# Gated linear attention with a feed-forward layer on one core: gate logits through their 16 columns, and five mended waits and passes

## The reference

```
q, k, v = x @ Wq, x @ Wk, x @ Wv          # 4 heads, 64 features for q and k, 128 for v
gl = x @ gk_w1 @ gk_w2 + gk_b             # gk_w1 256x16, gk_w2 16x256
g = log_sigmoid(gl) / 16
S = exp(gt)[:, None] * S + kt[:, None] * vt[None, :];  o_t = qt @ S     # scan over tokens
o = o * rsqrt(mean(o * o) + EPS) * rms_w;  o = o * silu(x @ Wg);  return o @ Wo
x = x + layernorm(attn(layernorm(x)))
x = x + layernorm(gelu(layernorm(x) @ w1 + b1) @ w2 + b2)
```

## Time and profile before

| what | value |
|---|---|
| median of 3 runs | 1352.19 us (1351.74 to 1352.67) |
| the profiled execution | 1351.44 us, its span 1349.6 us |
| PE busy | 1214.3 us (90%) |
| DVE busy | 1040.2 us (77%) |
| ACT busy | 735.0 us (54%) |
| POOL busy | 641.1 us (48%) |
| granted TensorE clock, mean | 0.964 of full speed |
| a pair of passes in the middle | 160.3 us (from 465.19 to 625.55 at the same step) |

### The profile page before, as it was taken

How to read it: one execution, slowest core, us unless ns; L and a number is a source line. 1 busy time by engine, 2 the same in 40 slices (tenths; PEclk the granted TensorE clock), 3 DMA queues, 4 the chain that set the end, 5 groups by cost and what they waited for, 6 DMA issues and landing times.

```text
span 1349.6 us, 24454 instructions
## 1 busy us (share of the span) xinstructions
PE 1214.3 (90%) x8644; PEld 1028.7 (76%) x8644; DVE 1040.2 (77%) x2436; ACT 735.0 (54%) x1571; POOL 641.1 (48%) x877
## 2 busy tenths in 40 slices
PE   5698998989989898998989899898998989999877
PEld 4577787868878787887878778786887868878766
DVE  3759687797868869688786978779686886968773
ACT  5364646656475565646556464665546555474423
POOL 5346353564435544554445635356444554545441
PEclk9889899999999999999999999999998999999998
DMA  2100010100101001020011001010010100101000
GB/s 94 36 32 17 1 56 9 51 17 17 48 1 53 15 17 47 5 63 1 17 48 52 17 0 55 10 52 16 17 48 1 52 17 17 48 1 52 1 17 16
DMA packets 31784, 38.34 MB, mean 28 GB/s; under 512 B 2448, under 2 KB 29104, under 8 KB 31664
## 3 DMA queue, kind: packets, MB, share of 16 engines
q1 hardware_dynamic: 31136, 36.25, 8.3%
q10 hardware_dynamic: 528, 0.52, 0.1%
HBM read 28.38 MB, written 8.39 MB: 27 GB/s over the span
## 4 chain that ended last, share of the span: by engine, by line
PE 47%; DVE 25%; POOL 10%; issue 10%; ACT 8%; DMA 0%; DVEq 0%; POOLq 0%; SPq 0%; ACTq 0%
PE ps_big L262 6%; PE ps_level L262 5%; PE ps_big L263 5%; DVE q_blockdiag L645 5%; PE ps_big L264 5%; PE ps_level L263 5%; PE ps_level L264 5%; DVE attn_T L615 4%; POOL rstd L1197 4%; PE ps_out L476 3%; PE ps_out L480 3%; ACT attn_T L941 3%; DVE o L684 2%; POOL x_mid L1203 2%; ACT ps_transpose L949 2%
## 5 line engine op out<-in xcount | busy, mean ns | idle before, releaser
L1191 POOL TENSOR_TENSOR k_decayed<-k_decayed,block_totals 128x256 f32<-128x256 f32 x192 | 167.5, 879 | 193.2 <-PE ps_level L309 114.9
L1197 POOL TENSOR_TENSOR rstd<-rstd,minus_half 128x1 f32<-128x1 f32 x192 | 118.0, 614 | 282.9 <-DVE rstd L697 282.7
L645 DVE TENSOR_TENSOR q_blockdiag<-q_blockdiag,block_totals 128x512 f32<-128x512 f32 x192 | 169.1, 887 | 29.7 <-PE ps_level L309 24.4
L262 PE MATMUL ps_level<-w_ff_hi,h_hi 128*128 128x256 f32 x512 | 148.6, 290 | 0.0
L264 PE MATMUL ps_level<-w_ff_hi,h_lo 128*128 128x256 f32 x512 | 144.7, 283 | 0.0
L263 PE MATMUL ps_level<-w_ff_lo,h_hi 128*128 128x256 f32 x512 | 144.7, 283 | 0.0
L302 PE MATMUL ps_level<-q_blockdiag,k_decayed 128*128 128x128 f32 x1024 | 132.0, 280 | 11.2 <-DVE attn_T L615 9.3
L302 PEld LDWEIGHTS ps_level<-q_blockdiag,k_decayed 128*128 128x128 f32 x1024 | 123.8, 193 | 16.6 <-DVE q_blockdiag L645 10.9
L987 ACT ACTIVATE square_out<-o 128x128 bf16<-128x128 f32 x256 | 76.0, 299 | 102.4 <-DVE o L662 102.3
L949 ACT ACTIVATE ps_transpose<-ps_big,ff_b_cols 128x512 f32<-128x512 f32 x128 | 84.6, 661 | 77.2 <-DVE h_lo L650 38.8
L262 PE MATMUL ps_big<-xT_hi,w_ff_hi 128*128 128x512 f32 x256 | 118.0, 461 | 3.2 <-DVE xT_lo L604 1.4
(11 more groups left out here) (142 smaller groups left out, 3415.1 us busy)
## 6 DMA issues: line engine op xcount, KB each, us to landing
w_raw<-L_ffn_w SPq DMA_DIRECT2D x16, 1024.0 KB, 6.2
out<-y SPq DMA_DIRECT2D x16, 512.0 KB, 3.1
x_in<-L_attn_x SPq DMA_DIRECT2D x15, 512.0 KB, 3.9
ff_b_rows<-L_ffn_b SPq DMA_DIRECT2D x8, 128.0 KB, 2.1
x_in<-L_attn_x ACTq DMA_DIRECT2D x1, 512.0 KB, 4.1
w_raw<-L_attn_Wv SPq DMA_DIRECT2D x1, 512.0 KB, 5.5
w_raw<-L_attn_Wg SPq DMA_DIRECT2D x1, 512.0 KB, 6.4
y<-L_attn_Wo SPq DMA_DIRECT2D x1, 512.0 KB, 7.4
```

Source lines behind the costliest of these rows:

```text
L262: nc.tensor.matmul(out, ah, bh, start=(first and i == 0), stop=False)
L645: nc.vector.tensor_tensor(q, q, t.to_broadcast([P, 2, T // (2 * h), h]), ALU.mult)\
L1191: nc.gpsimd.tensor_tensor(k, k, t.to_broadcast([P, n, h]), ALU.mult)\
L1197: nc.gpsimd.tensor_tensor(rs[:, k, c:c + 1], rs[:, k, c:c + 1], mhalf[:, 0:1], ALU.pow)\
```

## The change

1. Gate logits. `gl` now goes through the 16 columns: `gd` multiplies x by the thin first matrix with four matmuls 128x512, whose 128 output rows are four bands of 32 rows that hold the same 16 columns (three times the rounded weights, once the weights' rest). ACT rounds the result into `gate_lowrank`, DVE replaces band 2 by what rounding dropped (`lowrank_lo`, 32 rows), and `gl(0)`, `gl(1)` are one matmul each with the second matrix, stacked by rows in the same way. The small matrices are made at the start (five transfers ahead of the others, three clears on POOL, three ACT and two DVE operations on at most 256 elements); the old product matrix goes.
2. `gd` stands ahead of `kh`, and `gl` behind `att(0)`.
3. `level(6, tl)` waits for `ac_cp` at `4 * (tl + 1)`.
4. `att(c)`: the product of q and the state uses all 128 rows (the other head's q rows are zeros) and all four heads go to `ps_out`. `wo(2)` uses the other half of that bank.
5. Level 0: no copy to `qk_pair`; two masked copies of 512 elements straight from `ps_state`, one for each pair of heads, the second behind `q_update(4, 0)`. `q_update(4, 1)` moves ahead of `copy_pairs(4, 0)`.
6. `ogt(3)` moves ahead of `qp(1)`, `og_hi(3)` ahead of `q_blocks(0)` on ACT, `og_lo(3)` between the two `q_evac` on DVE, and `ln2(2)` ahead of `ln3(0)`.

```
@@ PE, level
-                            pe.wait_ge(sem["ac_cp"], at("ac_cp", s, 6 * tl + 4))
+                            pe.wait_ge(sem["ac_cp"], at("ac_cp", s, 4 * (tl + 1)))
@@ PE
+                def gd():
...
+                    for kt in range(KT):
+                        nc.tensor.matmul(PB[0][:, :], G1[0][:, kt, :], xT_hi[:, kt, :], start=(kt == 0), stop=False)
+                        last = nc.tensor.matmul(PB[0][:, :], G1[1][:, kt, :], xT_lo[:, kt, :], start=False,
+                                                stop=(kt == KT - 1))
+                    last.then_inc(sem["pe_gd"], 1)
                 def gl(tl):
...
+                    if tl == 0:
+                        pe.wait_ge(sem["dv_gr"], at("dv_gr", n, 1))
...
-                    feature_tile(PB[tl], 2 * D + tl * P).then_inc(sem["pe_gl"], 1)
+                    nc.tensor.matmul(PB[tl][:, :], G2[:, tl * P:(tl + 1) * P], gr[:, :], start=True, stop=True)\
+                        .then_inc(sem["pe_gl"], 1)
@@ PE, att
-                        for hh in range(2 if c else 0):
-                            r = slice(hh * HK, (hh + 1) * HK)
-                            last = nc.tensor.matmul((PO, PS)[hh][:, w], qbd[r, tl, hh, c * CH:(c + 1) * CH],
-                                                    S[r, tl, :], start=False, stop=True)
+                        if c:
+                            last = nc.tensor.matmul(PO[:, w], qbd[:, tl, hh, c * CH:(c + 1) * CH],
+                                                    S[:, tl, :], start=False, stop=True)
@@ DVE
+                def lowrank_lo():
+                    dve.wait_ge(sem["ac_gr"], at("ac_gr", n, 1))
+                    r = slice(2 * GB, 3 * GB)
+                    nc.vector.tensor_tensor(gr[r, :], PB[0][r, :], gr[r, :].bitcast(F32), ALU.subtract)\
+                        .then_inc(sem["dv_gr"], 1)
@@ ACT, behind the xT_hi copies and weight_hi
+                if A:
+                    act.wait_ge(sem["pe_gd"], at("pe_gd", n, 1))
+                    copy(gr[:, :], PB[0][:, :], "ac_gr")
@@ PE, end of a pass
                 if A:
                     gp(1, n)
                     qp(0)
+                if B:
+                    ogt(3)
+                if A:
                     qp(1)
                 if B:
                     wo(2)
-                    ogt(3)
@@ SP, at the start
-            sp.dma_start(w1t, w1t_d).then_inc(c_w[0], 16)
-            sp.dma_start(w2g, w2g_d).then_inc(c_w[0], 16)
+            sp.dma_start(w1s, w1g_d.rearrange("(k p) r -> p k r", p=P)).then_inc(c_g, 16)
+            sp.wait_ge(c_zero, 1)
+            for b in range(P // GB):
+                sp.dma_start(kT[b * GB:b * GB + LR, 1, :], w2g_d).then_inc(c_g, 16)
```

More of the change, by code:

```diff
@@ L82, in build @@
         h_hi, h_lo = sb("h_hi", [P, FT, T], F32R), sb("h_lo", [P, FT, T], F32R)
-        NA = 3 * D
-        WA = [sb(f"w_qkg_{n}", [P, KT, NA], F32R) for n in ("hi", "lo")]
+        NA = 2 * D
+        WA = [sb(f"w_qk_{n}", [P, KT, NA], F32R) for n in ("hi", "lo")]
+        G1 = [sb(f"w_gate_down_{n}", [P, KT, P], F32R) for n in ("for_hi", "for_lo")]
+        G2 = sb("w_gate_up", [P, D], F32R)
+        gr = sb("gate_lowrank", [P, T], F32R)
         WB = [sb(f"w_vg_{n}", [P, KT, 2 * DV], F32R) for n in ("hi", "lo")]
@@ L167, in build @@
         c_bias = ctx.enter_context(nc.semaphore("const_bias_in"))
-        c_w = [ctx.enter_context(nc.semaphore(f"const_{n}_in")) for n in ("gate", "qk", "vg", "o")]
+        c_w = [ctx.enter_context(nc.semaphore(f"const_{n}_in")) for n in ("qk", "vg", "o")]
+        c_g = ctx.enter_context(nc.semaphore("const_gate_in"))
+        c_zero = ctx.enter_context(nc.semaphore("const_gate_zero"))
+        c_ghi = ctx.enter_context(nc.semaphore("const_gate_hi"))
+        c_glo = ctx.enter_context(nc.semaphore("const_gate_lo"))
         c_ready = ctx.enter_context(nc.semaphore("const_ready"))
@@ L265, in three @@
                 return last
[L267 to L272, removed]
             pe.wait_ge(c_ready, 1)
@@ L538, in run @@
                     kh(1)
+                    st(0)
+                    att(0)
                 if A:
@@ L541, in run @@
                     gl(1)
-                if B:
-                    st(0)
-                    att(0)
                 if C:
@@ L868, in run @@
                         dve.wait_ge(c_bias, 32)
-                        const_lo(2)
+                        const_lo(1)
+                    lowrank_lo()
                     gates(0)
@@ L906, in run @@
                     q_evac(0)
+                if B:
+                    og_lo(3)
+                if A:
                     q_evac(1)
@@ L909, in run @@
                         dve.wait_ge(c_ready, 3)
-                        const_lo(3)
+                        const_lo(2)
                 if B:
+                    ln2(2, s)
                     ln3(0, s)
-                    ln2(2, s)
-                    og_lo(3)
                     ln3_stats(1, s)
@@ L1102, in run @@
                 if A:
+                    q_blocks(0)
                     q_blocks(1)
@@ L1122, in select @@
                 count[0] += 1
+            nc.gpsimd.memset(w2s, 0.0).then_inc(c_zero, 1)
+            for g in G1:
+                nc.gpsimd.memset(g[:, :, :].bitcast(F32), 0.0).then_inc(c_zero, 1)
             fill(mhalf[:, :], -0.5)
```

133 lines of the change are left out of this document (72 added, 61 removed).

## The result

The changed kernel takes 1337.2 us (1334.1 to 1339.3, 4 runs), against 1352.4 (1351.7 to 1353.2, 4 runs): a ratio of 0.989, 95% interval 0.986 to 0.991. It is faster, clear of the noise, but by 15 us (1.1%) and not by 59, and outside the range of 1281 to 1317. In the profiled execution the span is 1334.3 us and the mean granted clock 0.975.

The account below looks back on a forecast made before the run. PE, busy 90% of the span, was taken as the bound, with DVE or ACT sharing it in stretches of a pass. Savings of 38 + 9 + 12 + 0 - 0.5 = 59 us gave 1293 us, range 1281 to 1317.

Parts of the forecast that it names:

- Part 4: End of a pass: the 1.2 us wait at the last `wo` becomes 0.7 at `ogt(3)`; counted 0, at most 8 us gained.
- the dear state products: Rival at `att(c)`: full-array state products cost 0.5 us more per chunk, 24 us slower, 1329 us; chance 0.02.
- my sum: All parts: 38 + 9 + 12 + 0 - 0.5 = 59 us saved, giving 1293 us.
- Part 1: PE's wait at `level(6, 1)` for ACT's `attn_T` goes: 38 us saved, less level 0's new order; bounds 5 us.
- the new order of level 0: Level-0 copies in halves: DVE idles 0.65 us before `h_lo(0)` in even passes; about 0.1 lost in odd ones.
- Part 2: Gate logits, `gd` to `f2(2)`: PE takes 4.40 us for 5.02, gaining 0.6 us in 15 passes, 9 us.
- the room at `ogt(1)`: Between `og(1)`'s end and `ogt(1)`: 1.5 us of room, PE 1.2 us earlier; may just bind, so 12 of 15 us.
- the late logits bind: Rival: DVE and POOL can't follow, parts 2 and 3 bring nothing, only level 6 counts: 1314 us; chance 0.14.
- Part 3: State products in `att(c)` over the full array: 0.31 us gained in each of 48 chunks, 12 us taken; bounds 0 to 18.
- Part 5: Kernel start: more transfers, clears and a delayed `lowrank_lo` make it 0.5 us slower, bounds 2 either way.
- The clock's forecast: PE's mean granted clock rises from 0.964 to above 0.975, as the drop behind level 6 goes.

Follow-up runs that it names:

- number 3: The changed kernel with PE's new order kept, only `og_hi(3)` on ACT and `og_lo(3)` with `ln2(2)` on DVE back at their old places: 1303.7 us.
- number 8: The kernel before with only the state products in `att` over all 128 rows, into `ps_out` alone: 1342.0 us.
- kernel 1: The changed kernel with the end of a pass in its old order on PE, ACT and DVE: 1295.8 us.
- number 7: The kernel before with only the wait of level 6 changed, to the fourth and eighth copy: 1308.9 us.
- number 10: The changed kernel with the old end of a pass and level 0 back as one copy in its old place and order: 1297.3 us.
- number 11: The kernel before with only level 6's wait and the whole state products changed: 1296.9 us.
- number 9: The kernel before with only the gate logits and their start changed: 1350.9 us.
- numbers 1 and 5: Number 1 is kernel 1; number 5 is the changed kernel, order as changed, with a second buffer for chunks 1 and 3 of the gated output: 1298.5 us.

## Why the prediction was wrong

**Part 4, the end of a pass, is the step that failed:** "I count 0; bounds 0 to 0.5 us a pass", with a gain as the far bound. It cost 2.3 to 2.8 us a pass by the markers (pairs of 158.0 to 159.0 against 153.4 to 153.5 us) and 6 us more behind the last marker, where `wo(2)` stands behind the 3.61 us wait of `ogt(3)` (number 3): 41 us in all. In seven passes a part of it is clock: a stretch at the lower level begins 0.2 to 1.5 us behind the 1.95 us hole at `level(1, 0)`, and such passes are 0.2 to 0.7 us longer than their like. I had looked at `ogt(3)` and its wait for `og(3)`, and that was right: 0.7 forecast, 0.66 measured, and the 18.0 us at the last `wo` are gone. What I left out is what the moved `og_hi(3)` itself waits for and what is queued behind it. The rows on the place show `ogt(3)`; of `og_hi(3)` I used no row, and its second wait stands in the code of `og_hi`, one line below the first. No rival had a loss in this part; the one nearest in time, the dear state products at 1329, is out by number 8. Without this part my sum is that of kernel 1, 1293 against 1295.8, but that agreement has luck in it: level 6 is worth more than I counted and the gate logits less, as follows.

**Part 1, level 6:** forecast 38, with the new order of level 0 counted in; the wait alone won 43, and its own working says 44 (number 7). The mechanism was right. The mis-sized term is level 0: the even pass's 0.65 us for DVE's idle time came true (`0.55` ahead of `h_lo(0)`), but the odd passes give as much back (0.77 lost, 0.83 won, numbers 10 and 11), so the term should have been nearly 0 for a pair. The two half copies of level 0 take 1.31 us each, for 1.24 assumed:

```profile
684.64 0.69 DVE L674 TENSOR_TENSOR h_lo<-ps_transpose,h_hi 128x512 fp32r<-128x512 f32 x1 [0.55 <-ACT h_hi L980]
...
686.28 1.31 DVE L659 COPY_PREDICATED attn_T<-level_masks,ps_state 128x512 f32<-128x512 uint32 x1
```

**Part 2, the gate logits:** forecast 9, measured 1 alone (not clear of noise) and none beside parts 1 and 3. PE's own sum was right: from `gd` to `f2(2)` it takes 4.30 us (4.40 forecast, 5.02 before), the wait for `k_tokens` 0.52 of it. Alone, the clock ate it (number 9). Beside parts 1 and 3, what was lost is the room at `ogt(1)`. I wrote "So it may just bind" and charged 3 us of 24 for it; it binds for 0.5 us in each pass, and the rival "the late logits bind" was right for this part and wrong for part 3.

**Part 3, the state products:** forecast 12, measured 10. `att(1)` takes 639.13 - 637.33 = 1.80 us (1.82 forecast):

```profile
637.33 0.49 PE L493 MATMUL ps_out<-v,attn_T 128*128 128x128 f32 x2
637.65 0.39 PE L496 MATMUL ps_out<-state,q_blockdiag 128*128 128x128 f32 x2
...
639.13 0.36 PE L270 MATMUL ps_level<-w_ff_hi,h_hi 128*128 128x256 f32 x1
```

The rule of the Trainium skill ("TensorE: Matmul & The Clock Gate", section on packing small matmuls), by which the untiled products would cost, is not borne out by these fp32 products of 64 rows: four heads take 1.80 us untiled and 2.13 in pairs, and the edit alone, with its change of bank, wins 10 us.

**Part 5, the start,** was not timed by itself. From the first marker to the third the kernel of number 10 takes 135.2 us and that of number 11, without the new logits and their start, 133.3; number 9 takes 139.4 and the kernel before 135.5. So the start, with the first passes' logits, costs some 2 to 4 us there for 0.5 forecast. The clock's forecast (above 0.975) was not quite met: 0.974 to 0.977 in the four runs, 0.975 in the profiled one, and 0.983 to 0.986 in kernel 1. No low-clock stretch appeared in `f2` behind the holes of level 5.

## What to carry to other kernels

When a step moves forward, list everything that the moved instruction waits for, the reader of its own output buffer above all, and who stands behind it in its queue: with one buffer, a copy for chunk c can't go ahead of the product of chunk c-1, wherever its input is. Of a saving on the bound engine, ask at once which side chain it makes later; here 0.67 us saved were given back at a wait two stages on, and moving two matmuls and one VectorE step forward brought them in. And an edit that moves the time little may be several edits: here one of the parts ate 41 us of the 56 that the others brought.

## What the runs showed of the hardware

A stretch at the lower clock costs nothing where the engine would wait next anyway, and its full price behind the wait: in the kernel before, in an odd pass, it lay at 616.6 to 620.0 us, with a hole behind it; with 0.67 us less work in a pass it lay behind the hole, cost 1.6 us, and the gain was gone (number 9). With the hole of level 6 gone and no other of its size (numbers 1 and 5), all of passes 2 to 14 ran at the full clock in `f1`, and passes of one parity agree within 0.2 us. Numbers 10 and 11 have the same two holes at level 5 of an odd pass (0.73 and 1.23 us). Number 10 had a low-clock stretch in `f1` behind them in two passes, which made these 0.2 to 0.4 us longer, and number 11 had none; so the size of the holes alone doesn't tell where the clock falls. Halving the level-0 copy cost 2 x 1.31 = 2.62 us for 2.48 in one, read from PSUM instead of SBUF; the small copy of 0.16 us that it made needless pays for that. By the start of the step behind, a half takes 1.10 us (686.28 to 687.38) and the whole 2.27 (688.41 to 690.68 in the kernel before).
